# Four-batch attention with a routed feed-forward layer: VectorE's program nested in its branches, tile weights moved by transfers, name marks made on VectorE, expert work from step 53

## The chip, the cores and the metric

The kernel runs on one core of a Trainium2 chip. The metric is the device time of one execution in microseconds (us), smaller is better. The times shown are a median of three runs; one further execution was recorded by the hardware profiler, and every row below is from that one.

## The reference

Four sequences of 1024 tokens, 128 features each, go through a layer norm. The result is used twice, and both uses are added to the input.

```
xn  = layernorm(x)                                   # x is 4 x 1024 x 128
# attention, 16 heads of 8 features
Q, K = rope(xn @ W_q.T), rope(xn @ W_k.T);  V = xn @ W_v.T
attn = softmax(Q K^T / sqrt(8));            a = (attn V) @ W_o.T
# feed-forward: 8 experts, each token takes its 2 best
w, idx = top_k(xn @ Wg, 2);  w = softmax(w)
h_e   = relu((xhat * gamma_e + beta_e) @ W1_e + b1_e)     # 128 -> 512
out_e = h_e @ W2_e + b2_e + xn                            # 512 -> 128
y     = sum over the two experts of w * out_e
return x + a + y
```

## The kernel before, in words

The attention is a loop of 256 **steps**, counted by n: 4 batches of 64 steps, each batch 4 **quads** of 16 steps (a quad is four heads), each quad two halves of 8 steps (512 queries), and a step takes one block of 128 keys. In step n TensorE computes the scores of step n + 1 (line L631, into `sc`), then one piece of other work, called an **aside**, and then weighs the values with the exponentials of step n (L665, into `acc`). ScalarE does the two exponentials of each step (L879, into `ring`). At every step that 8 divides VectorE runs `tail`: it transposes `acc` (L1048) and so releases it; the weighing of that step waits for this. VectorE's own part of the asides, in the order of `aside(n)`, comes behind the tail. Each engine runs its program strictly in the order written, and all PSUM traffic of the asides goes through one bank, `aside_bank`, one piece at a time, by the counters `bank_full` and `bank_taken`.

Which aside stands at which step is a table of numbers. Up to step 26 the asides prepare the values and the routing. Then `mark` (VectorE, L1180 and L1182) makes one-hot matrices for the routing in 8 groups; GpSimd multiplies the narrow one by row and pair names (`named`, L456 and L458); `invert` on TensorE (L692) turns each group into part of a list, which VectorE adds up (`take_named`, L1190 and L1193); `tokens` (L1199 to L1212) makes from the list the numbers of the rows that each of the 71 tiles of 128 token slots gathers. From step `FFN_FROM` on two asides serve one tile: `layer_one` (TensorE L710, VectorE `relu` L1251) and `layer_two` (TensorE L699 for the next tile's transpose and L720, VectorE `rows_out` L1258 with `columns` L1245). They are spread evenly over the steps up to 236, apart from steps that other asides take. A tile's weights (1158 floats a partition: two matrices, biases, gamma and beta) are copied by VectorE from `w_all`, where all experts lie, into one of three buffers `w_tile` in the memory of `xn` (L1240; the expert's number is read into a register at L1237). GpSimd gathers the token rows (L483) and scatters the results (L493) by indirect transfers, and adds up and splits the rotated projections of the next batch (`split`, L466 to L472), which ScalarE squares for a bound (L885). SyncE loads the score operands of the next quad (`load_stack`, L310).

The bound decides, once for a batch, whether the slow path with row maxima is needed; with these inputs it never is. TensorE's program is nested: the fast path of all batches stands in a row, the slow paths behind it. VectorE's before has a test ahead of every quad, which jumps over `maxima` when the path is fast: 16 taken branches.

## Time and profile before

| | us |
|---|---|
| median of 3 runs | 644.51 (643.55 to 647.97) |
| the profiled execution, its own time | 650.07 |
| its span, first to last instruction | 648.2 |

The profiled execution is 5.56 us longer than the median. Sums are made against it, and then carried to the median.

### The profile page before, as it was taken

Reading aid. Unit: us, or ns where it says so; the run is one execution under the profiler, and the core shown is the slowest. Engines: PE = TensorE matmul, PEld = TensorE weight load, DVE = VectorE, ACT = ScalarE, POOL = GpSimd, SP = SyncE. Lnnn points to the kernel's source line nnn. Section 1 sums busy time; section 2 is a strip of 40 time slices with the busy share of each in tenths; the row PEclk is TensorE's granted clock in tenths of the full one; section 3 lists DMA queues with packets and bytes.
Section 4 is the critical chain, followed back from the end, with each engine's and each line's share of the span. In section 5 each row is a group of like instructions: output and inputs, shape, how many; then the busy total and the mean of one; then the engine's idle time right before and its main releaser. Section 6 shows DMA issues by size and latency. Waiting matters only on the chain.

```text
span 648.2 us, 12158 instructions
## 1 busy us (share of the span) xinstructions
PE 574.3 (89%) x4620; PEld 242.5 (37%) x4620; DVE 358.3 (55%) x1057; ACT 504.7 (78%) x552; POOL 277.5 (43%) x319
## 2 busy tenths in 40 slices
PE   8899865898999999899989999989998999989783
PEld 6233111234444444244434444434433544434111
DVE  4965879565554444667545444466654445334661
ACT  3799976777788888678857888777876888868991
POOL 4399547599643233456422323336632323311000
PEclk9999989889999999899979999999998999989996
DMA  6167310001101101000120100100022011110720
GB/s 233 34 184 210 98 34 1 4 22 54 55 22 45 34 25 50 18 17 26 50 54 18 51 29 25 50 17 22 22 58 51 21 54 26 35 37 10 295 84 18
DMA packets 25362, 35.48 MB, mean 55 GB/s; under 512 B 5440, under 2 KB 15728, under 8 KB 24784
## 3 DMA queue, kind: packets, MB, share of 16 engines
q1 hardware_dynamic: 19936, 23.70, 11.9%
q0 software_dynamic: 4544, 9.32, 5.3%
q10 hardware_dynamic: 816, 1.61, 0.7%
q8 instruction: 39, 0.64, 0.4%
q14 instruction: 27, 0.22, 0.1%
HBM read 17.36 MB, written 8.85 MB: 40 GB/s over the span
## 4 chain that ended last, share of the span: by engine, by line
PE 68%; DVE 15%; ACT 9%; issue 4%; DMA 2%; another core or an unknown queue 1%; ACTq 1%; POOL 0%; DVEq 0%
PE acc L665 27%; PE aside_bank L710 12%; PE aside_bank L720 10%; PE sc L631 10%; ACT ring L879 9%; PE aside_bank L699 3%; DVE work L1251 2%; DVE blocks L1048 2%; DVE xn L1240 2%; PE aside_bank L558 2%; PE aside_bank L729 2%; DMA sin<-rope_sin 1%; DVE rotated L1221 1%; PE aside_bank L542 1%; DVE turned L921 1%
## 5 line engine op out<-in xcount | busy, mean ns | idle before, releaser
L879 ACT ACTIVATE ring<-sc 128x1024 f32<-128x1024 f32 x512 | 490.6, 1039 | 112.8 <-PE sc L631 96.6
L665 PE MATMUL acc<-ring,v 128*9 128x512 f32 x2048 | 275.3, 608 | 51.3 <-DVE blocks L1048 33.1
L483 POOL DMA_INDIRECT work<-normed,token x71 | 71.9, 1013 | 230.5 <-DVE work L1245 224.9
L1251 DVE TENSOR_SCALAR work<-aside_bank,xn 128x128 f32<-128x128 f32 x284 | 80.0, 344 | 124.8 <-PE aside_bank L710 113.8
L631 PEld LDWEIGHTS sc<-qs,ks 32*128 32x128 f16 x1024 | 25.9, 91 | 230.9 <-ACT ring L879 180.7
L631 PE MATMUL sc<-qs,ks 32*128 32x512 f16 x1024 | 102.9, 390 | 4.0 <-ACT ring L879 2.0
L493 POOL DMA_INDIRECT token_out<-work,token x71 | 72.9, 1027 | 45.2 <-DVE work L1245 22.3
L710 PE MATMUL aside_bank<-work,xn 128*128 128x128 f32 x568 | 82.7, 289 | 2.0 <-DVE rotated L1221 2.0
L720 PE MATMUL aside_bank<-xn,work 128*128 128x128 f32 x568 | 77.4, 280 | 0.0
L710 PEld LDWEIGHTS aside_bank<-work,xn 128*128 128x128 f32 x568 | 69.4, 192 | 18.6 <-issue 18.6
L720 PEld LDWEIGHTS aside_bank<-xn,work 128*128 128x128 f32 x568 | 73.9, 202 | 0.3 <-DVE work L1251 0.3
L665 PEld LDWEIGHTS acc<-ring,v 128*9 128x9 f32 x2048 | 30.7, 88 | 102.8 <-DVE blocks L1048 31.7
L1240 DVE COPY xn<-w_all 128x1158 f32 x71 | 62.7, 883 | 0.3 <-issue 0.3
L1258 DVE TENSOR_TENSOR work<-aside_bank,xn 128x128 f32<-128x128 f32 x71 | 20.7, 291 | 70.8 <-PE aside_bank L720 70.8
L1048 DVE STREAM_TRANSPOSE blocks<-acc 128x512 f32<-128x512 f32 x32 | 22.8, 711 | 24.2 <-PE acc L665 22.8
L1245 DVE TENSOR_SCALAR work<-aside_bank,xn 128x128 f32<-128x128 f32 x71 | 28.5, 402 | 1.5 <-PE aside_bank L699 1.5
L699 PE MATMUL aside_bank<-const,work 128*128 128x128 f32 x71 | 22.2, 313 | 4.1 <-DMA work<-normed,token 2.1
L456 POOL TENSOR_SCALAR xn<-xn,const 128x568 bf16<-128x568 bf16 x8 | 15.6, 1955 | 23.7 <-DVE xn L1182 23.7
L921 DVE SCALAR_TENSOR_TENSOR turned<-aside_bank,gain,cos 128x512 f32<-128x512 f32 x13 | 9.7, 749 | 16.9 <-PE aside_bank L558 16.9
L451 POOL TENSOR_SCALAR xn<-xn,small 128x128 f32<-128x128 f32 x32 | 18.6, 605 | 0.1
L699 PEld LDWEIGHTS aside_bank<-const,work 128*128 128x128 f32 x71 | 10.0, 140 | 21.4 <-issue 12.0
L466 POOL TENSOR_TENSOR turned<-turned,rotated 128x512 f32<-128x512 f32 x12 | 15.9, 1326 | 0.2
(185 smaller groups left out, 369.0 us busy)
## 6 DMA issues: line engine op xcount, KB each, us to landing
w_all<-L_ffn_W SPq DMA_DIRECT2D x16, 256.0 KB, 4.8
qs<-hl SPq DMA_DIRECT2D x60, 64.0 KB
ks<-hl SPq DMA_DIRECT2D x60, 64.0 KB
x<-L_attn_x SPq DMA_DIRECT2D x4, 512.0 KB, 8.3
normed<-xn SPq DMA_DIRECT2D x4, 512.0 KB, 3.3
xn<-token_out SPq DMA_DIRECT2D x2, 1024.0 KB, 5.8
w_all<-token_out SPq DMA_DIRECT2D x2, 1024.0 KB, 10.9
out<-x SPq DMA_DIRECT2D x8, 256.0 KB, 2.2
```

Source lines behind the costliest of these rows:

```text
L483: pool.indirect_dma_start(out=xt[t % TILE_BUFFERS], out_offset=None, in_=xh_d[:, :], in_offset=bass.IndirectOffsetOnAxis(ap=token[:, 0, t: ...
L493: pool.indirect_dma_start(out=y_d[:, :], in_=ys[done % TILE_BUFFERS], in_offset=None, out_offset=bass.IndirectOffsetOnAxis(ap=token[:, 1, ...
L631: last = nc.tensor.matmul(dst, ks[r:r + 32, kb * P:(kb + 1) * P], qs[r:r + 32, at], start=True, stop=not slow)
L665: last = nc.tensor.matmul(acc[32 * j:32 * j + VW, :], v9[:, b, kb, 4 * g + j, :], ring[:, (2 * n + j // 2) % UNITS, j % 2, :], start=(kb = ...
L699: return nc.tensor.transpose(bank[0][:, D:D + P], xt[t % TILE_BUFFERS], ident)
L710: last = nc.tensor.matmul(bank[0][:, c * P:(c + 1) * P], w_tile[t % 3][:, c * P:(c + 1) * P], xsT[t % 2], start=True, stop=True)
L720: last = nc.tensor.matmul(bank[0][:, 0:D], hT[t % 2][:, c, :], w_tile[t % 3][:, W2_AT + c * D:W2_AT + (c + 1) * D], start=(c == 0), stop=( ...
L879: nc.scalar.activation(ring[:, (2 * n + u) % UNITS, :, :], sc[score_pair(2 * n + u)][:, :].rearrange("p (h c) -> p h c", h=2), ACT.Exp, sc ...
L1048: nc.vector.transpose(blocks[:, :, :].rearrange("p q r -> p (q r)"), acc[:, :]).then_inc(acc_out, 1)
L1240: nc.vector.tensor_copy(w_tile[t % 3], w_all[:, bass.ds(e, 1), :].rearrange("p o w -> p (o w)")).then_inc(w_ok, 1)
L1245: return nc.vector.tensor_scalar(xsT[t % 2], bank[0][:, D:D + P], w_tile[t % 3][:, GA_AT:GA_AT + 1], w_tile[t % 3][:, BE_AT:BE_AT + 1], AL ...
L1251: last = nc.vector.tensor_scalar(hT[t % 2][:, c, :], bank[0][:, c * P:(c + 1) * P], w_tile[t % 3][:, B1_AT + c:B1_AT + c + 1], 0.0, ALU.ad ...
```

## The change

Five things are changed together.

1. VectorE's program gets the nesting that TensorE's has: with the fast path, no branch is taken between the start and the end of the loop, and one far jump stands at its end. The flag of the next batch is read after step 62 of the batch, by TensorE too (it was 61).
2. VectorE's copies of the tile weights are gone. SyncE reads the expert's number and issues a transfer from `w_all` into `w_tile`: three at step 49 (steps are counted as above), then the one of tile t + 3 at the step of `layer_two(t)`.
3. GpSimd's `named` products are made by VectorE, behind each `mark`.
4. The table is new: experts from step 53 (48), `invert` at 34 to 49 (33 to 44), `tokens` at 49 (45), `gates` at 46 (26), and small moves of projections and bounds.
5. The same number of expert asides (142) goes into 184 steps in place of 189.

```diff
-ROUTE_AT, RANKS_AT, SLOTS_AT, GATES_AT = 21, 24, 24, 26
-INVERT_AT = {33 + (3 * g + 1) // 2: g for g in range(GROUPS)}
+ROUTE_AT, RANKS_AT, SLOTS_AT, GATES_AT = 21, 24, 24, 46
+INVERT_AT = {n: g for g, n in enumerate((34, 36, 39, 41, 43, 45, 47, 49))}
-TOKENS_AT = 45
-PLAIN_AT = {n: (1, r) for r, n in enumerate((37, 43, 46, 50))}
+TOKENS_AT = 49
+PLAIN_AT = {n: (1, r) for r, n in enumerate((38, 44, 48, 51))}
-BRANCH_AT = 61
+BRANCH_AT = 62
-FFN_FROM, FFN_TO = 48, 237
-NORM_AT = {PER_BATCH * b - 8: b for b in range(1, B)}
-FLAG_AT = {PER_BATCH * b - 6: b for b in range(1, B)}
+FFN_FROM, FFN_TO = 53, 237
+NORM_AT = {PER_BATCH * b - 6: b for b in range(1, B)}
+FLAG_AT = {PER_BATCH * b - 4: b for b in range(1, B)}
-SQUARE_AT.update({n: (1, r) for r, n in enumerate((50, 51, 53, 55))})
+SQUARE_AT.update({n: (1, r) for r, n in enumerate((50, 55, 56, 57))})
-WEIGHTS_AT = {n: t + 2 for n, t in FIRST.items() if t + 2 < SLOT_TILES}
+WEIGHTS_AT = {n: t + 3 for n, t in SECOND.items() if t + 3 < SLOT_TILES}
...
+            def weights(t):
+                e = sp.value_load(owner[0:1, t:t + 1], min_val=0, max_val=E - 1)
+                if t >= 3:
+                    sp.wait_ge(bank_taken[0], USE["two", t - 3])
+                sp.dma_start(w_tile[t % 3], w_all[:, bass.ds(e, 1), :].rearrange("p o w -> p (o w)")
+                             ).then_inc(w_in[t % 3], 16)
...
+                    if n == TOKENS_AT:
+                        sp.wait_ge(exp_in, 16 * 3 * E)
+                        sp.wait_ge(owner_ok, 1)
+                        sp.wait_ge(bank_taken[0], USE["invert", GROUPS - 1])
+                        for t in range(3):
+                            weights(t)
+                    if n in WEIGHTS_AT:
+                        weights(WEIGHTS_AT[n])
...
-            for g in range(GROUPS):
-                k, js = g % 2, slice(GROUP * g, GROUP * (g + 1))
-                pool.wait_ge(mark_ok, g + 1)
-                nc.gpsimd.tensor_scalar(named[k][:, :, 0, :], tile_mark[k], row_name, None, ALU.mult
-                                        ).then_inc(named_ok, 1)
-                nc.gpsimd.tensor_tensor(named[k][:, :, 1, :], tile_mark[k],
-                                        pick_name[:, js].unsqueeze(2).to_broadcast([P, GROUP, SLOT_TILES]), ALU.mult
-                                        ).then_inc(named_ok, 1)
...
-                pe.wait_ge(named_ok, 2 * (g + 1))
...
-                pe.wait_ge(w_ok, t + 1)
+                pe.wait_ge(w_in[t % 3], 16 * (t // 3 + 1))
...
+                link(nc.vector.tensor_tensor(tile_mark[k], iota_t[:, 0:SLOT_TILES].unsqueeze(1).to_broadcast(shape),
+                                             slot_hl[:, 0, js].unsqueeze(2).to_broadcast(shape), ALU.is_equal))
+                nc.vector.tensor_scalar(named[k][:, :, 0, :], tile_mark[k], row_name, None, ALU.mult)
+                nc.vector.tensor_tensor(named[k][:, :, 1, :], tile_mark[k],
+                                        pick_name[:, js].unsqueeze(2).to_broadcast(shape), ALU.mult
                                         ).then_inc(mark_ok, 1)
...
-            def weights(t):
-                e = v.value_load(owner[0:1, t:t + 1], min_val=0, max_val=E - 1)
-                if t >= 3:
-                    v.wait_ge(bank_taken[0], USE["two", t - 3])
-                nc.vector.tensor_copy(w_tile[t % 3], w_all[:, bass.ds(e, 1), :].rearrange("p o w -> p (o w)")
-                                      ).then_inc(w_ok, 1)
...
-            for b in range(B):
-                v.wait_ge(flag_ok, b + 1)
-                fast = v.value_load(flag[0:1, b:b + 1], min_val=0, max_val=1)
+            def attend(b, slow):
+                following = None
                 for n in body_steps(b):
-                    if (n + 1) % PER_QUAD == 0:
-                        with v.If(fast == 0):
-                            maxima((n + 1) // PER_QUAD)
+                    if slow and (n + 1) % PER_QUAD == 0:
+                        maxima((n + 1) // PER_QUAD)
                     if n >= 0:
                         aside(n)
+                    if not slow and n == PER_BATCH * b + BRANCH_AT and b + 1 < B:
+                        following = flag_of(b + 1)
+                return following
...
+            def batches(b, fast):
+                links = chain[0]
+                with v.If(fast == 1):
+                    following = attend(b, False)
+                    if b + 1 < B:
+                        batches(b + 1, following)
+                chain[0] = links
+                with v.Else():
+                    for later in range(b, B):
+                        attend(later, True)
```

Three places of the program, before and after. The first is VectorE behind the slots, where the first two groups are marked. `small` belongs to `gates`, `xn` holds the marks, `wide_q` to `mrow` are the slow path. Before:

```order
L1120 TENSOR_SCALAR small<-small 128x32
L1180 TENSOR_TENSOR xn<-const,slot_hl 128x1024
L1182 TENSOR_TENSOR xn<-const,slot_hl 128x568
L1180 TENSOR_TENSOR xn<-const,slot_hl 128x1024
L1182 TENSOR_TENSOR xn<-const,slot_hl 128x568
L1339 COMPARE_AND_BRANCH
L1029 TENSOR_SCALAR wide_q<-qs,missing 128x1024
L1030 CAST wide_k<-ks 128x1024
L1033 TENSOR_REDUCE mx<-sc 128x1 x32
L1036 TENSOR_SCALAR mrow<-sc 32x128
L1039 TENSOR_SCALAR mrow<-mrow 32x128
L1042 TENSOR_TENSOR mrow<-mrow 32x128
```

After:

```order
L1177 CAST slot_hl<-slot_i 128x128
L1188 TENSOR_TENSOR xn<-const,slot_hl 128x1024
L1190 TENSOR_TENSOR xn<-const,slot_hl 128x568
L1192 TENSOR_SCALAR xn<-xn,const 128x8x71
L1193 TENSOR_TENSOR xn<-xn,const 128x8x71
L1188 TENSOR_TENSOR xn<-const,slot_hl 128x1024
L1190 TENSOR_TENSOR xn<-const,slot_hl 128x568
L1192 TENSOR_SCALAR xn<-xn,const 128x8x71
L1193 TENSOR_TENSOR xn<-xn,const 128x8x71
L1055 STREAM_TRANSPOSE blocks<-acc 128x512
```

The seven `small` instructions of the gates have gone to step 46, two products stand behind each pair of marks, and the tail (the last row) follows without the slow path between.

The second is VectorE in an expert step ahead of a tail, at step 103 before (`work` is the relu's output, `owner` the expert's number):

```order
L1251 TENSOR_SCALAR work<-aside_bank,xn 128x128 x4
L1237 TENSOR_LOAD owner
L1237 ISA x2
L1240 ISA
L1240 COPY xn<-w_all 128x1158
L1048 STREAM_TRANSPOSE blocks<-acc 128x512
L1051 RECIPROCAL rec<-blocks 128x16
L1052 TENSOR_TENSOR att<-blocks,rec 128x16x8
```

After, at the same tail:

```order
L1255 TENSOR_SCALAR work<-aside_bank,xn 128x128 x4
L1262 TENSOR_TENSOR work<-aside_bank,xn 128x128
L1249 TENSOR_SCALAR work<-aside_bank,xn 128x128
L1055 STREAM_TRANSPOSE blocks<-acc 128x512
L1058 RECIPROCAL rec<-blocks 128x16
L1059 TENSOR_TENSOR att<-blocks,rec 128x16x8
```

The read of the owner and the copy are gone; here the second layer's two instructions stand ahead of the tail.

The third is SyncE after step 54 (`qs` and `ks` are the score operands of the next quad). Before, these transfers follow one another with only tests between:

```order
L310 DMA qs<-hl 32x1024 x4
L310 DMA ks<-hl 32x1024 x4
L365 TENSOR_LOAD flag
L365 ISA x2
L369 COMPARE_AND_BRANCH
```

After:

```order
L351 DMA xn<-w_all 128x1158
L311 DMA qs<-hl 32x1024 x4
L311 DMA ks<-hl 32x1024 x4
L348 TENSOR_LOAD owner
L348 ISA x2
L351 ISA
L351 DMA xn<-w_all 128x1158
```

The weights' transfers now stand in SyncE's program between the loads for the quads, in order with them.

## Rows read from the trace of the kernel before

**Rows 1.** Three stretches: start:end, length, busy us (x count) by engine, clock, DMA, GB/s.

```profile
0.00:143.60 143.60, 120.04 (x905) 44.62 (x906) 101.71 (x363) 109.34 (x136) 94.93 (x128) 0.96 0.31 92
143.60:599.00 455.40, 422.55 (x3472) 190.86 (x3476) 232.74 (x618) 360.31 (x378) 182.34 (x192) 0.98 0.13 35
599.00:648.20 49.20, 31.67 (x249) 7.05 (x248) 23.82 (x77) 35.04 (x38) 0.27 (x1) 0.88 0.34 131
```

**Rows 2.** Chain of waits in time order: start, length, what.

```profile
354.12 1.09 PE aside_bank L710 x8
359.04 1.09 PE aside_bank L710 x8
...
599.06 27.59 ACT ring L879 x30
```

**Rows 3.** Groups by line from 0 to 143.6 us: busy, mean ns, idle before.

```profile
L879 ACT ACTIVATE ring<-sc 128x1024 f32<-128x1024 f32 x106 | 100.5, 1050 | 19.1 <-PE sc L631 16.0 <-issue 2.7
...
L710 PE MATMUL aside_bank<-work,xn 128*128 128x128 f32 x16 | 2.9, 340 | 0.3 <-DVE rotated L1221 0.3
```

**Rows 4.** Who waited for whom from 143.6 to 599 us: total, times, longest.

```profile
PE acc L665 <- DVE blocks L1048: 24.3, 15, 2.8
```

**Rows 5.** VectorE's groups by shape, whole span.

```profile
L1240 DVE COPY xn<-w_all 128x1158 f32 x71 | 62.7, 883 | 0.3 <-issue 0.3
...
L1182 DVE TENSOR_TENSOR xn<-const,slot_hl 128x568 bf16<-128x568 f32 x8 | 8.7, 1093 | 0.0
```

**Rows 6.** Timeline of VectorE and TensorE around the first marks, 84 to 114 us.

```profile
84.54 0.17 DVE L1114 TENSOR_SCALAR small<-small 128x32 f32<-128x32 f32 x1
...
86.01 1.22 DVE L1180 TENSOR_TENSOR xn<-const,slot_hl 128x1024 bf16<-128x1024 f32 x1
87.15 0.74 DVE L1182 TENSOR_TENSOR xn<-const,slot_hl 128x568 bf16<-128x568 f32 x1
...
89.60 0.71 DVE L1048 STREAM_TRANSPOSE blocks<-acc 128x512 f32<-128x512 f32 x1
...
90.37 1.90 PE L665 MATMUL acc<-ring,v 128*9 128x512 f32 x8 [3.72 <-DVE blocks L1048]
...
113.12 1.30 PE L665 MATMUL acc<-ring,v 128*9 128x512 f32 x8 [3.93 <-DVE blocks L1048]
```

**Rows 7.** Timeline: TensorE's first expert tile waits for its gather.

```profile
130.41 0.30 PE L699 MATMUL aside_bank<-const,work 128*128 128x128 f32 x1 [2.09 <-DMA work<-normed,token]
```

**Rows 8.** Timeline: ScalarE's square of batch 1, last piece.

```profile
152.79 0.63 ACT L885 ACTIVATE xn<-turned 128x512 bf16<-128x512 f32 x1 [2.38 <-POOL turned L466]
```

**Rows 9.** Timeline: a weight copy ahead of a tail, and the weighing behind it.

```profile
268.06 1.90 DVE L1240 COPY xn<-w_all 128x1158 f32 x1
...
270.64 1.81 PE L665 MATMUL acc<-ring,v 128*9 128x512 f32 x8 [2.35 <-DVE blocks L1048]
```

**Rows 10.** Timeline at the start of batch 2, behind VectorE's branch.

```profile
327.69 1.16 PE L710 MATMUL aside_bank<-work,xn 128*128 128x128 f32 x8
...
330.45 1.13 DVE L1251 TENSOR_SCALAR work<-aside_bank,xn 128x128 f32<-128x128 f32 x4 [3.35 <-remote]
...
332.97 1.90 PE L665 MATMUL acc<-ring,v 128*9 128x512 f32 x8 [2.82 <-DVE blocks L1048]
```

**Rows 11.** Timeline at the start of batch 3, and at step 224.

```profile
492.24 1.54 PE L665 MATMUL acc<-ring,v 128*9 128x512 f32 x8 [2.00 <-DVE blocks L1048]
...
570.08 1.94 ACT L879 ACTIVATE ring<-sc 128x1024 f32<-128x1024 f32 x2 [2.45 <-remote]
```

**Rows 12.** TensorE's branches: ns min/median/max, first and last start.

```profile
L809 PEldq COMPARE_BRANCH  x5: 71/73/3279, 22.5 to 632.5; - x5
```

**Rows 13.** DMA issues: KB each, us from issue to landing.

```profile
xn<-token_out SPq DMA_DIRECT2D x2, 1024.0 KB, 5.8
...
ks<-hl ACTq DMA_DIRECT2D x2, 32.0 KB, 2.1
```

**Rows 14.** Timeline: VectorE near the end.

```profile
640.88 0.72 DVE L1048 STREAM_TRANSPOSE blocks<-acc 128x512 f32<-128x512 f32 x1 [10.99 <-PE acc L665]
```

More of the change, by code:

```diff
@@ L271, in build @@
         v_one, shift_zero, xh_out, ws_ok = (sem(n) for n in ("v_one", "shift_zero", "xh_out", "ws_ok"))
-        halves_ok, mark_ok, named_ok, token_ok = (sem(n) for n in ("halves_ok", "mark_ok", "named_ok", "token_ok"))
+        halves_ok, mark_ok, token_ok = (sem(n) for n in ("halves_ok", "mark_ok", "token_ok"))
         wqk_tr, wv_tr, wT_ok, wvg_ok, wo_sorted = (sem(n) for n in ("wqk_tr", "wv_tr", "wT_ok", "wvg_ok", "wo_sorted"))
@@ L284, in build @@
                                                                          "owner_ok"))
-        base_ok, w_ok, merged, out_ok = (sem(n) for n in ("base_ok", "w_ok", "merged", "out_ok"))
+        base_ok, merged, out_ok = (sem(n) for n in ("base_ok", "merged", "out_ok"))
+        w_in = [sem(f"w_in{k}") for k in range(3)]
         y_home = [sem(f"y_home{b}") for b in range(B)]
@@ L344, in _ @@
                 sp.dma_start(w_all[:, e, B2_AT:B2_AT + D], b2_d[e:e + 1, :].to_broadcast([P, D])).then_inc(exp_in, 16)
+            def weights(t):
[4 more added lines that the diff above has]
+                             ).then_inc(w_in[t % 3], 16)
             def load_outputs():
-                sp.wait_ge(w_ok, SLOT_TILES)
+                for k in range(3):
+                    sp.wait_ge(w_in[k], 16 * len(range(k, SLOT_TILES, 3)))
                 for k in range(TILE_BUFFERS):
@@ L1177, in mark @@
                     bank_is_full(0, "invert", g - 2)
+                    v.wait_ge(mark_ok, g - 1)
                 k, js = g % 2, slice(GROUP * g, GROUP * (g + 1))
@@ L1312, in aside @@
                 if n == FFN_FROM - 1:
-                    v.wait_ge(exp_in, 16 * 3 * E)
-                    v.wait_ge(owner_ok, 1)
-                    weights(0)
                     bank_is_full(0, "tile")
                     columns(0).then_inc(bank_taken[0], 1)
-                    weights(1)
                 if n in FIRST:
@@ L1322, in aside @@
                     rows_out(SECOND[n])
-                if n in WEIGHTS_AT:
-                    weights(WEIGHTS_AT[n])
                 if n in SINE_AT:
```

8 lines of the change are left out of this document (5 added, 3 removed).

## The prediction, made before the changed kernel ran

> **What bounds the kernel now.** I read the stretches first [rows 1]. From 143.6 to 599 us, the expert part, TensorE is busy 422.6 of 455.4 us (93%), VectorE only 232.7 and ScalarE 360.3: TensorE sets the pace. The chain of waits gives that pace: two steps of an expert tile take 359.04 - 354.12 = 4.92 us, 2.46 a step [rows 2]. Without expert work ScalarE sets it: 30 exponentials, 15 steps, in 27.59 us, 1.84 a step [rows 2]. So an expert aside costs 2.46 - 1.84 = 0.62 us wherever it stands, and 142 of them cost the same in 184 steps as in 189. VectorE's 62.7 us of weight copies [rows 5] therefore lie almost wholly beside TensorE's work, and most of what the change removes is worth nothing. What can be won is in places where TensorE stands still for VectorE: at the tails, 24.3 us in 15 waits in the expert part [rows 4], and more before it [rows 6].
>
> **Steps 32 to 52, where the table is new.** ScalarE has done 106 exponentials by 143.6 us, so step 53 begins there, and TensorE by then has begun two expert tiles (16 L710 records are two first layers) [rows 3]; by the table two second layers are behind it or running too. The weighing of step 32 waited 3.72 us for its tail, that of step 40 3.93 us, both times with VectorE deep in marks [rows 6]; the first tile waited 2.09 us for its gather [rows 7]. Now the same with the new order, with durations of rows:
> - A mark is 1.22 + 0.74 us when nothing disturbs it [rows 6], less some 0.1 of overlap. The two products are not on VectorE in this trace. The nearest row for the one of two tensors is L1182, same size, 0.74; for the one with a scalar between a third of that and 0.74, I take 0.4. With the wait between, a mark with names is 3.1 us (2.9 to 3.5). Before, beside GpSimd's products, L1182 took 1.09 in the mean against 0.74 [rows 5]; that disturbance goes, since GpSimd is then idle.
> - First tail: the gates, 84.54 to 86.01, move away (-1.5), two pairs of products come in (+2.5): the transpose starts near 90.7, not 89.60 [rows 6]. That is 1.1 us lost.
> - Later: mark plus `take_named` is 3.4 us, against two steps of 3.68. VectorE keeps up except where a projection with its sine (2.2 us) or a tail (1.3) falls between. I followed the three engines through steps 33 to 52 with these numbers. TensorE waits some 3 us at step 40 (as now), 1.3 near 46, 1.5 near 49, and a few tenths elsewhere. It no longer waits for GpSimd's chain of products. Step 53 begins near 138.5, 5.0 us earlier. Of this the four expert asides that had been done before and now are not, 4 x 0.62 = 2.5 us, must be given back later. Net -2.5.
> - Start of the expert part: tokens to first tile is now three steps, not two, so the 2.09 us wait [rows 7] would go (it is in the 5.0 above). But the gathers now meet three weight transfers of 593 KB. I charge +1.0 (0 to +4). Sum of this part: -1.5 us.
>
> **The square.** ScalarE stood 2.38 us for GpSimd's sum of the last projection of batch 1 [rows 8], since that split came two rounds of gathers and scatters late. The new table runs all three splits in round 3 and squares at step 57: -2.4.
>
> **Copies that collide ahead of a tail.** The copy at 268.06 took 1.90 us [rows 9], against a mean of 0.88 over all 71 [rows 5]; GpSimd's split ran at the same time, and I take the two to disturb each other; the tail stands behind it and TensorE 2.35 us behind that, then at a lower clock for a step (1.81 against 1.05 us) [rows 9]. The same happens once a batch later. Without the copy the transpose starts right behind the relu: -2.3 and -1.2, together -3.5.
>
> **VectorE's taken branches.** There are 16. At the start of batch 2 the relu starts at 330.45 where TensorE was through by 327.69 + 1.16 = 328.85: 1.6 us late, then a copy (0.76) and the tail; TensorE waits 2.82 and runs slow for one and a half steps [rows 10]. I put that at 3.8: the wait of 2.82, 0.85 on the first weighing (1.90 against 1.05), the rest on slow scores. Batch 3 has the same with a wait of 2.00 [rows 11]: 1.9. At the other 14 I find no late start of VectorE. So nesting pays at two of 16: -5.7 with the clock, of which the copies are a part. At its end the new program has one far jump. TensorE's took 3.28 us [rows 12]. VectorE has nothing to do for 10.99 us before its last transpose [rows 14], so I cost the jump at nothing; without that cover it would be +3.3.
>
> The Trainium skill ("Runtime: NRT & Kernel Launch", Instruction fetch mechanics) says that a taken branch stalls when its target is outside the two pages that are held. By that rule, the trace agrees: the far jump shows, most short ones don't. The rule speaks against the change, since 14 of the 16 branches that go were cheap and the one that comes is far; a sum that paid 1.6 us for each of 16 would give 22 us more than mine.
>
> **Copies ahead of other tails.** 24.3 us in 15 waits, less the 2.35, 2.82, 2.00 and their likes, leaves tails at which 0.76 of a copy was partly in the way: about -1.2. The step where both ScalarE and VectorE stood until 570 us, 2.45 us [rows 11], has no releaser that I can name. I leave it (0, range to -3).
>
> **The transfers.** 593 KB a tile. Bounds from rows: 32 KB landed in 2.1 us, 1024 KB in 5.8 [rows 13]; I take 4. A transfer goes out when `layer_two(t)` is taken and is asked for by `columns(t + 3)` two tiles later, 9.8 us. SyncE may be busy with eight loads of a quad in between, but these are there once in 16 steps. So it hides. The added traffic is 593 KB per about 5.1 us, 115 GB/s beside 35 [rows 1]. Gathers have three tiles in hand. I charge +1.0 for the whole (0 to +6).
>
> The Trainium skill ("DMA: Bandwidth & Descriptors", Issuing engines are not separate DMA queues) says that transfers of all issuing engines run on the same 16 DMA engines and interleave. By its fit (Anatomy of one DMA, 2.0 us plus bytes at 436 GB/s, for GpSimd's path) one of 593 KB is an estimated 3.4 us; the sum would be the same by it. No trace here has both streams together.
>
> **Sum.** -1.5 - 2.4 - 3.5 - 5.7 - 1.2 + 1.0 = -13.3 us. Against the profiled execution's own 650.07 that is 636.8. The median is 5.6 us shorter than that execution, so some of its stalls are probably not in every run; 644.51 - 13.3 = 631.2, and I give back a little: **632.0**. With the bounds: all of it, 570 us too and 2 us more from the table, 625; table nothing, branches half, transfers +6, about 642.
>
> **Rivals.**
> - *The weights come late.* Three buffers: a buffer is in use for one tile (4.92 us) and then waits for issue (0.6) and landing. A round of three tiles takes 14.76 us, so it decides from a landing of 9.2 us on. At 10.3 us every tile takes (10.3 + 0.6 + 4.92) / 3 = 5.27 us, 0.35 more; over 68 tiles 24 us, less the gain: 656. For: never has this core moved such a stream beside gathers and score loads. Against: 1024 KB landed in 5.8 [rows 13], and DMA load is 13% [rows 1]. Chance 0.07.
> - *VectorE becomes the bound in steps 32 to 52.* If the products take 1.09 each, as L1182 in the mean, every mark costs 0.8 to 1.0 more, eight marks 7 us, most of it seen. Together with a clock that drops after each stall: 639. Chance 0.12.
> - *The stalls are of the profiled execution.* If the two branch stalls and the clock dips are rare in plain runs, -5.7 falls to -1 and the collisions stay: 637 to 641. Chance 0.13.
> - *More than forecast:* the stall at 570 belonged to the branch or to a fetch of VectorE's, and the table gives its 5 us in full: 626. Chance 0.12.
> - *Every taken branch costs, hidden by other waits.* Were each of the other 14 worth the 1.6 us of batch 2 [rows 10], 22 us more would go: 610. The timeline, where 14 don't show, speaks against. Chance 0.02.
>
> **How the numbers follow.** The forecast (628 to 637) has 0.54. Range 624 to 643: it holds the forecast, the second, third and fourth rival, 0.91 by this list and less in truth, since the hand-followed part may be off by 3 us either way. 1% is about what a measurement of this kernel can tell from no change: below 638.1 is faster. Faster: 0.54 + 0.12 + 0.02 + half of the second and third (0.12) = 0.78. Within 1%: 0.14. Slower: the late weights, and something like a reaction of the clock, 0.08.
>
> **What would show each step.** Step 53's exponentials (the 107th) near 138 to 139 us; the tail of step 32 near 91; VectorE's products near 0.4 and 0.74 us and L1182's kin at 0.74 throughout; no wait of ScalarE for GpSimd's sum; relus of steps 127 and 191 within 0.1 us of TensorE's end; total wait of the weighing for tails in the expert part near 12 us instead of 24; weights landing in 3 to 6 us, no wait of TensorE or VectorE for them except at the first tile; the last transpose unmoved by VectorE's far jump. Wrong it would be if expert steps took more than 2.46 us all along, or if the first tile waited 5 us for gather or weights.

## The result, and the profile after

The changed kernel takes 619.88 us (618.98 to 620.08, 4 runs), against 644.70 (643.55 to 647.97, 4 runs) for the kernel before, run beside it: ratio 0.960, 95% interval 0.957 to 0.963. The gain is 24.8 us; the forecast was 12.5 and the range ended at 624. The profiled execution took 618.98, its span is 617.1.

The stretches of the kernel after, cut where [rows 1] are cut: at step 53's and step 237's first exponential. Columns: stretch, us, busy us of PE, PEld, DVE, ACT, POOL, clock, DMA share, GB/s.

```profile
0.00:139.10 139.10, 117.55 (x878) 41.08 (x878) 97.56 (x364) 108.29 (x135) 58.09 (x98) 0.95 0.33 101
139.10:571.50 432.40, 418.49 (x3498) 191.25 (x3502) 181.80 (x562) 358.89 (x379) 188.40 (x206) 1.00 0.37 132
571.50:617.10 45.60, 30.05 (x248) 6.92 (x248) 23.82 (x77) 35.05 (x38) 0.25 (x1) 0.91 0.36 142
```

Against [rows 1] the first stretch is 4.5 us shorter, the expert part 23.0 (455.4 to 432.4), and the end 3.6. TensorE does nearly the same work in the expert part (418.5 us busy, 422.6 before) and is now busy 97% of it. So the gain is idle time of TensorE. The wait of [rows 4] (24.3 us, 15 times) has almost gone; here are the three largest waits of TensorE in the expert part after (who waited for whom, total, times, longest). There is none for weights, only one for the first gather. The largest, for VectorE's relu, stands in the step behind a tail in four of its five places.

```profile
PE aside_bank L706 <- DVE work L1255: 3.7, 5, 1.5
PE acc L673 <- DVE blocks L1055: 2.6, 5, 0.5
PE aside_bank L706 <- DMA work<-normed,token: 1.6, 1, 1.6
```

The first marks, in the place of [rows 6], VectorE and TensorE:

```profile
84.75 1.23 DVE L1188 TENSOR_TENSOR xn<-const,slot_hl 128x1024 bf16<-128x1024 f32 x1
85.89 0.74 DVE L1190 TENSOR_TENSOR xn<-const,slot_hl 128x568 bf16<-128x568 f32 x1
86.67 0.37 DVE L1192 TENSOR_SCALAR xn<-xn,const 128x568 bf16<-128x568 bf16 x1
86.95 0.74 DVE L1193 TENSOR_TENSOR xn<-xn,const 128x568 bf16<-128x568 bf16 x1
...
90.47 0.71 DVE L1055 STREAM_TRANSPOSE blocks<-acc 128x512 f32<-128x512 f32 x1
...
91.23 1.90 PE L673 MATMUL acc<-ring,v 128*9 128x512 f32 x8 [4.46 <-DVE blocks L1055]
```

The reader sees the products at 0.37 and 0.74, and the transpose of step 32 at 90.47; the estimates were 0.4, 0.74 and 90.7.

### The profile page after: what moved, and what is told of

It reads as the page before. It is cut to its first block, busy times and chain, and to the rows that moved or that the text cites. A ratio compares the mean times of both kernels' runs of the same rounds, so it can differ in the third digit from the quotient of the medians.

```text
span 617.1 us, 12160 instructions
## 1 busy us (share of the span) xinstructions
PE 566.1 (92%) x4620; PEld 239.3 (39%) x4620; DVE 303.2 (49%) x1002; ACT 502.2 (81%) x552; POOL 246.7 (40%) x303
## 4 chain that ended last, share of the span: by engine, by line
PE 72%; ACT 13%; DVE 9%; issue 4%; DMA 1%; ACTq 0%; DVEq 0%
PE acc L673 28%; ACT ring L886 13%; PE aside_bank L717 12%; PE sc L639 10%; PE aside_bank L727 10%; PE aside_bank L706 3%; PE aside_bank L566 2%; PE aside_bank L736 2%; DVE work L1255 1%; DVE blocks L1055 1%; PE aside_bank L550 1%; DVE xn L1188 1%; DVE rotated L1232 1%; PE sc L566 1%; DMA wr<-L_attn_W_k 1%
## 5 line engine op out<-in xcount | busy, mean ns | idle before, releaser
L673 PE MATMUL acc<-ring,v 128*9 128x512 f32 x2048 | 271.4, 602 | 26.2 <-ACT ring L886 12.1
L501 POOL DMA_INDIRECT token_out<-work,token x71 | 71.1, 1001 | 42.4 <-DVE work L1249 19.4
L727 PE MATMUL aside_bank<-xn,work 128*128 128x128 f32 x568 | 75.1, 275 | 0.0
L727 PEld LDWEIGHTS aside_bank<-xn,work 128*128 128x128 f32 x568 | 71.4, 196 | 0.3 <-DVE work L1255 0.3
L673 PEld LDWEIGHTS acc<-ring,v 128*9 128x9 f32 x2048 | 30.5, 88 | 76.1 <-ACT ring L886 25.9
L566 PE MATMUL aside_bank<-xnT,wT 128*128 128x512 f32 x26 | 14.5, 641 | 1.4 <-DVE work L1204 0.8
L480 POOL TENSOR_TENSOR hl<-turned,hl 128x512 f16<-128x512 f32 x12 | 14.0, 1167 | 1.0
```

The lines of the kernel that those rows point to most:

```text
L501: pool.indirect_dma_start(out=y_d[:, :], in_=ys[done % TILE_BUFFERS], in_offset=None, out_offset=bass.IndirectOffsetOnAxis(ap=token[:, 1, ...
L566: return nc.tensor.matmul(dst, wT[:, k, :], xnT[:, b * S + c * CH:b * S + (c + 1) * CH], start=True, stop=True)
L673: last = nc.tensor.matmul(acc[32 * j:32 * j + VW, :], v9[:, b, kb, 4 * g + j, :], ring[:, (2 * n + j // 2) % UNITS, j % 2, :], start=(kb = ...
L727: last = nc.tensor.matmul(bank[0][:, 0:D], hT[t % 2][:, c, :], w_tile[t % 3][:, W2_AT + c * D:W2_AT + (c + 1) * D], start=(c == 0), stop=( ...
```

## The experiments

Fifteen kernels in four sets, each set with runs of the kernel before on its own chip. Medians of before were 646.97, 642.76, 642.22 and 642.04, so ratios carry across sets better than times. The changed kernel itself ran in none of the four sets: a difference from it in us, taken from two medians, can be off by some 3 us, and where the ratios give another number it stands beside. A single profile varies too. Its first exponential comes at 23.2 to 28.2 us in the 17 profiles, by nothing that was changed, and the expert part took 432.4, 432.1 and 429.4 us in three kernels with the same program there (after, branches_back, after_landing_142_on). One word on lines: where a kernel has more or fewer lines ahead of a place, the same instruction has another number (L665, L673 and L682 are the same weighing).

### One part undone

Each is the changed kernel with one part as it was.

**copies_back**

```diff
-                sp.dma_start(w_tile[t % 3], w_all[:, bass.ds(e, 1), :].rearrange("p o w -> p (o w)")
-                             ).then_inc(w_in[t % 3], 16)
...
+                nc.vector.tensor_copy(w_tile[t % 3], w_all[:, bass.ds(e, 1), :].rearrange("p o w -> p (o w)")
+                                      ).then_inc(w_ok, 1)
```

The waits for the weights and the steps at which they are asked for go back with it.

> The changed kernel with the weight copies back on VectorE; the table, the nesting and the names stay as changed. Theory A (free steps): the kernel gained mainly because the new table has 5 free steps at tails where the old had 15 and 3 more taken by other asides; a copy matters only at the few tails that it stands ahead of. Then this costs 4 to 8 us: 624 to 628. Theory B (copies): the copies ahead of the tails were the cost, whatever the table: 12 us or more back, 632 or above. Theory C (transfers dear): the 593 KB transfers cost something themselves, so this is no slower than 620.

Measured: 625.62 (623.89 to 627.84), ratio 0.968 (0.962 to 0.973).

**branches_back**

```diff
-            batches(0, flag_of(0))
...
+                    if (n + 1) % PER_QUAD == 0:
+                        with v.If(fast == 0):
+                            maxima((n + 1) // PER_QUAD)
```

> The changed kernel with VectorE's 16 tests and jumps back; all else as changed. Forecast's step: two late relus with what hangs on them, so 3 to 6 us slower, 623 to 626. Rival: the late relus need the copy behind them to be seen by TensorE, and without copies the branches cost under 1 us each: below 622. Rival: the nesting is the large part, 10 us or more: 630 or above.

Measured: 619.32 (617.42 to 620.94), ratio 0.959 (0.954 to 0.967). Sixteen tests and jumps on VectorE are worth nothing that shows, as the first rival said.

**names_back**

```diff
-                nc.vector.tensor_scalar(named[k][:, :, 0, :], tile_mark[k], row_name, None, ALU.mult)
+                nc.gpsimd.tensor_scalar(named[k][:, :, 0, :], tile_mark[k], row_name, None, ALU.mult
+                                        ).then_inc(named_ok, 1)
...
```

The second product goes back in the same way.

> The changed kernel with the names back on GpSimd, table as changed. VectorE's marks get 1.0 us shorter but disturbed by GpSimd again. Theory of the trace: the tail of step 32 comes 2.2 us earlier, but groups wait for GpSimd's 2.9 us chain; the new table leaves two steps (3.7 us) to each group, so it is about even: 618 to 622. Rival (the names' move was needed): marks of 2.6 to 3.1 us and TensorE waiting for names, 623 or above.

Measured: 615.48 (612.19 to 616.51), ratio 0.952 (0.945 to 0.958). The third part of the change costs 4.4 us by the medians (5.4 by the ratios), against an expectation of about even: step 53 begins at 134.7 in place of 139.1. By ScalarE's starts, steps 33 to 52 take 46.2 us here and 50.0 to 52.2 in the five kernels with the new table and the products on VectorE.

**after_free_at_tails**

```diff
+AT_TAILS = (64, 80, 88, 96, 104, 120, 128, 144, 152, 160, 168, 184, 192, 208, 216, 224, 232)
...
-    due = (n + 1 - FFN_FROM) * 2 * SLOT_TILES
+    due = (n + 1 - FFN_FROM) * 2 * SLOT_TILES + 5 * (FFN_TO - FFN_FROM)
-    if n not in TAKEN and used * (FFN_TO - FFN_FROM) < due:
+    if n not in TAKEN and n not in AT_TAILS and used * (FFN_TO - FFN_FROM) < due and used < 2 * SLOT_TILES:
```

> The changed kernel, but the free steps of the expert part lie at the same 17 tails as before (5 others at the end); the number of expert asides is the same. Theory A (a free step at a tail is partly lost, since TensorE has nothing to do while VectorE transposes): without copies each costs some 0.5 us, 12 more of them than in the changed kernel, so 6 us: 625 to 627; with copies it would be some 1.0 each. Theory B (copies alone): no change, 619 to 621.

Measured: 621.22 (619.53 to 621.80), ratio 0.961 (0.955 to 0.967): 1.3 us by the medians, 0.5 by the ratios, which is no difference that can be told, and not the 5 or more of theory A. The expert part of its profile is 434.8 us, 2.4 to 5.4 more than in the three profiles named above.

What follows: no part undone gives back more than 6 us, though 24.8 were won. Either the parts stand in for one another, or the gain is in the table.

### One part alone

Each is the kernel before with one part changed.

**table_alone**: the numbers of the new table, nothing else. 

> The kernel before with the new table of steps alone: copies on VectorE, names on GpSimd, tests ahead of quads, all as before. From the first four runs: the changed kernel 619.9, copies back +5.7, names back -4.4, branches back -0.6; if the parts add, this is 620.6. Theory A (the table is the large part): 618 to 625, some 22 us below the kernel before. Theory B (parts stand in for each other, each hides the tail's wait): 630 to 636.

Measured: 618.50 (615.81 to 618.91), ratio 0.960 (0.957 to 0.963). The table alone gives the whole gain.

**before_tails_filled**: one line of the code that makes the table; a step that 8 divides always gets an expert aside, and others are left free in its place.

```diff
-    if n not in TAKEN and used * (FFN_TO - FFN_FROM) < due:
+    if n not in TAKEN and (used * (FFN_TO - FFN_FROM) < due or n % KB == 0 and used < 2 * SLOT_TILES):
```

> The kernel before with one line changed: a step that 8 divides always gets an expert asides, and the free step comes right behind it. No other change. Theory A (a free step at a tail is lost with the copy in the way): 15 free steps at some 0.8 us, 10 to 14 us faster: 631 to 635. Rival (the tail costs the same with or without an aside beside it, since VectorE's relu then stands behind the tail): no change, 643 to 646.

Measured: 623.74 (623.11 to 626.82), ratio 0.971 (0.968 to 0.974): 19 us by one line, where 10 to 14 were expected. It also moved the place at which TensorE's far jump lands, which is worth 3 of them (see "Behind the last loop step").

**transfers_alone**: the edit of copies_back the other way round. 

> The kernel before with the weights moved by SyncE's transfers alone; old table, names on GpSimd, tests as before. Three transfers at step 45 and the first tile at step 47, so the first weights may be waited for some 3 us. If the copies' cost lies in tails as the trace of before had it (24.3 us in 15 waits, less those that stay), 12 to 16 us faster: 629 to 633. If it is only what undoing it in the changed kernel cost, 5.7 less those 3: 640 to 643.

Measured: 628.21 (626.98 to 629.49), ratio 0.976 (0.974 to 0.979): 14.5 us, within the 12 to 16 of the first reading.

**nested_alone**: the edit of branches_back the other way round. 

> The kernel before with VectorE's program nested, nothing else. The forecast said 5.7 us for the two late relus with what follows. Theory A (they need a copy ahead of the tail to be seen, and here it is there): 3 to 6 us faster, 639 to 642. Rival (worth nothing here too, as in the changed kernel, and the late relus have another cause): 643 to 646.

Measured: 641.90 (640.12 to 642.51, 10 runs), ratio 0.997 (0.995 to 1.000): about 1 us, not 3 to 6.

**transfers_tails_filled**: both of the two large ones. 

> The fourth corner of a square: the kernel before with the weights by transfers (alone 628.2) and with its tails filled (alone 623.7). Theory A (both take away the same wait, of a weighing for a tail that stands behind a copy): without copies the filled tails bring 0 to 1.5 us in the expert part, which takes 428 to 430 us, and what else the fill brings is the place of TensorE's landing, 2.5 to 3.5 us: 623.5 to 626. Theory B (the two are independent terms of -14.5 and -19): 609 to 611.

Measured: 619.10 (617.17 to 620.21), ratio 0.964 (0.961 to 0.967). As independent terms the two would give 609; they share some 10 us. But theory A gave 623.5 to 626, so the filling still brings more with transfers (9 us, of which 3 are at the end, see below) than theory A allows.

The expert part of four of them, by stretches: nested_alone, before_tails_filled, transfers_alone, transfers_tails_filled.

```profile
144.86:589.53 444.67, 416.53 (x3472) 188.15 (x3476) 232.03 (x618) 360.34 (x378) 182.77 (x192) 1.00 0.13 36
```

```profile
144.90:576.00 431.10, 416.05 (x3472) 188.07 (x3476) 229.63 (x618) 358.55 (x379) 181.73 (x192) 1.00 0.13 37
```

```profile
147.40:577.20 429.80, 415.03 (x3472) 188.22 (x3476) 177.97 (x550) 359.75 (x379) 174.08 (x188) 1.00 0.36 129
```

```profile
147.50:571.60 424.10, 415.11 (x3472) 188.18 (x3476) 177.73 (x550) 358.45 (x378) 174.02 (x188) 1.00 0.37 131
```

The same TensorE work (415 to 416.5 us) in 444.7, 431.1, 429.8 and 424.1 us. Filling takes 13.6 off with copies and 5.7 with transfers; transfers take 14.9 off alone and 7.0 when the tails are filled. (The first of the four is nested_alone and not before, whose profiled execution had stalls of its own; the nesting is worth some 1 us.)

### Where the filled tail pays: step 80

The three steps 80 to 82 hold the same work everywhere: a tail, the second layer of tile 12, the first of tile 13, and one free step. The kernel before, with step 80 free:

```profile
209.93 1.13 DVE L1251 TENSOR_SCALAR work<-aside_bank,xn 128x128 f32<-128x128 f32 x4 [1.87 <-PE aside_bank L710]
...
210.97 0.75 DVE L1240 COPY xn<-w_all 128x1158 f32 x1
211.64 0.71 DVE L1048 STREAM_TRANSPOSE blocks<-acc 128x512 f32<-128x512 f32 x1
...
212.41 1.04 PE L665 MATMUL acc<-ring,v 128*9 128x512 f32 x8 [1.30 <-DVE blocks L1048]
```

TensorE has only scores to do between two weighings, and VectorE does relu, copy and transpose in a row. The wait is 1.30. The same with transfers:

```profile
212.14 1.13 DVE L1261 TENSOR_SCALAR work<-aside_bank,xn 128x128 f32<-128x128 f32 x4 [1.78 <-PE aside_bank L727]
...
213.18 0.70 DVE L1065 STREAM_TRANSPOSE blocks<-acc 128x512 f32<-128x512 f32 x1
...
213.94 1.05 PE L682 MATMUL acc<-ring,v 128*9 128x512 f32 x8 [0.54 <-DVE blocks L1065]
```

And with the copy where it was but the second layer moved onto the tail (before_tails_filled):

```profile
211.09 0.75 DVE L1240 COPY xn<-w_all 128x1158 f32 x1
...
211.41 1.06 PE L720 MATMUL aside_bank<-xn,work 128*128 128x128 f32 x8
211.76 0.71 DVE L1048 STREAM_TRANSPOSE blocks<-acc 128x512 f32<-128x512 f32 x1
...
212.52 1.05 PE L665 MATMUL acc<-ring,v 128*9 128x512 f32 x8
```

The second layer runs while VectorE copies and transposes, and TensorE's wait is gone. From ScalarE's starts, steps 80 to 82 take 7.52 us before (208.75 to 216.27), 6.75 with transfers (211.05 to 217.80) and 6.80 filled (208.96 to 215.76). In these three steps the size is that of the copy, by either way.

Over all places a second loss shows. ScalarE runs one step ahead, so what a free step n brings shows in the starts up to step n + 3. From n to n + 3 three expert steps take 7.3 us. With the free step n away from a tail they take 6.36, in nested_alone and in transfers_alone alike (10 places each). With the free step at a tail they take 6.76 in the mean with transfers (15 places), and with the copy 7.43 at the usual place, 7.65 in the mean, where the collisions of steps 105 and 169 are in it. So a free step brings 0.9 us elsewhere, 0.5 at a tail, and nothing at a tail behind a copy. The copy costs 0.67 there (0.73 in the mean of the first two steps, 11 us in 15), and the tail itself 0.40. The second is what filling still brings with transfers: 0.39 to 0.41 us in most of the stretches of eight steps whose tail was free (steps 80 to 87: 17.97 and 17.57), and 15 x 0.40 = 6.0 for the 5.7 measured.

### The table again, both ways

**table_alone_free_at_tails**: the edit of after_free_at_tails on table_alone. 

> The kernel before with the new table, but with the expert work's free steps held at the 17 tails at which an earlier table has no expert aside; copies on VectorE, names on GpSimd, tests ahead of the quads. With the new table as it stands this program took 618.5. Theory A (a free step is worth 1 us anywhere but at a tail that stands behind a copy, and 17 such tails lose it): the one line that filled the tails of the kernel before was worth 19 us, so taking them away again gives 634 to 638, with waits of the weighing for VectorE's blocks in the expert part of 15 us or more, and step 53 within 0.5 us of 134.6. Theory B (the gain of the table comes from the steps below 53, from the later gates, list and projections): 618 to 622, waits under 9 us.

Measured: 624.09 (622.15 to 626.38), ratio 0.970 (0.967 to 0.973): 5.6 us lost and not 15, step 53 at 135.2, the weighings' waits for VectorE's blocks up to 15.8 us in 19. Neither theory's number. ScalarE's starts say why: of the 17 free steps at tails only 6 now stand behind a first layer, whose relu the copy follows; from n to n + 3 they take 7.47 us in the mean. Ten stand behind a second layer, which has no copy, and take 6.73. (The last, 232, has another free step ahead.) In the kernel before all 15 stand behind a first layer. Against 6.36 elsewhere that is 6 x 1.11 and 10 x 0.37, 10.4 us, less 2.6 by the same count for the five free tails of table_alone: 7.8, where the expert parts of the two profiles differ by 7.2 (442.6 and 435.4). So a free tail costs 0.4, and behind a copy 1.1. I had counted tails and not what stands ahead of them.

**old_table**: the changed kernel with the numbers of before. 

> The changed kernel with the table of before: nesting, weights by transfers, names on VectorE, experts from step 48, 142 asides in 189 steps. Theory A (transfers already free most tails, the table does the rest): the transfers alone gave 628.2; names on VectorE add 3 to 5 us, since they lengthen the time to the first tail and stand ahead of the list; nesting takes 1: 629 to 634. Theory B (parts add up as separate terms, the table worth 24 us): 619.9 + 24 = 644.

Measured: 632.37 (630.39 to 633.26), ratio 0.984 (0.982 to 0.987), as theory A said. The table is worth 12.5 us in the changed kernel by the medians (some 16 by the ratios) and 24 in the kernel before. By stretches the two compare so: to step 53 148.6 and 139.1, expert part 430.1 and 432.4, behind it 49.9 and 45.6. With transfers, then, the table wins before step 53 and at the end, and in between nothing that is clear of what single profiles differ by: it has four more asides to do there, and ten fewer free steps at tails.

### The order of the marks

**names_back_mark_later** is names_back with one number more:

```diff
-MARK_AT = {27: 0, 28: 1}
+MARK_AT = {27: 0, 32: 1}
```

> The changed kernel with the name products back on GpSimd and the second mark moved from step 28 to step 32, where VectorE runs it behind the tail. With the products back alone it took 615.5. Theory A (the tail of step 32 stands behind two marks, TensorE waits 3 us or more for it, and ScalarE sets the pace below step 53, so that this wait shows in full): the weighing of step 32 no longer waits, step 53 begins 1.5 to 3 us earlier than 134.65, and the time is 612.5 to 614. Theory B (VectorE is short of time up to step 50 whatever the order, the second mark only comes late and the list with it): 615 to 617, with the wait moved to steps 36 to 41.

Measured: 608.63 (607.59 to 610.10, 5 runs), ratio 0.948 (0.945 to 0.950). Theory A's direction, and more than it said: 6.9 us below names_back by the medians, though 2.6 by the ratios. It is 11 us faster than the changed kernel by the medians, 8 by the ratios. The marks:

```profile
86.76 0.71 DVE L1065 STREAM_TRANSPOSE blocks<-acc 128x512 f32<-128x512 f32 x1
...
87.53 1.04 PE L682 MATMUL acc<-ring,v 128*9 128x512 f32 x8 [0.64 <-DVE blocks L1065]
...
89.26 1.68 DVE L1199 TENSOR_TENSOR xn<-const,slot_hl 128x568 bf16<-128x568 f32 x1
```

The weighing of step 32 waits 0.64 us, against 4.46 in the kernel after. L1199, the second operation of a mark, takes 1.68 with GpSimd beside it and not 0.74, yet that costs less than the two products did on VectorE. By ScalarE's starts, steps 33 to 52 take 41.9 us; in the kernel after 52.2, in names_back 46.2. In the next run, whose program is the same up to step 53, they take 43.3, so 3 to 4 us are the mark's.

**names_back_later_filled**: that with the tails filled too. 

> The same, and the expert asides never leave a tail free (the five tails 88, 96, 144, 184 and 232 are filled, and other steps are freed in their place). Theory A (a free step at a tail is lost only where the tail is late, and with transfers it hardly is): the five are worth 0 to 1.5 us, so 611.5 to 614. Theory B (a free step at a tail is worth nothing in any case): 5 us, so 608 to 610.

Measured: 608.50 (605.68 to 608.88, 6 runs), ratio 0.946 (0.943 to 0.948): no difference that can be told in the medians. In the profiles the expert part is 2.0 us shorter (430.3 and 428.3), five tails at 0.4, which is just above theory A's 0 to 1.5; steps 33 to 52 are 1.4 longer, where nothing was changed. The absolute times of both theories were built on too late a start. These two beat both kernels.

### Behind the last loop step

The end of the chain of waits in the kernel before, from the last exponential (columns: start, us, what):

```profile
634.28 1.56 issue
635.84 0.89 PE acc L665
636.73 2.19 issue
638.93 1.93 PE acc L665 x7
```

And after:

```profile
606.76 1.63 issue
608.39 1.22 PE acc L673 x8
```

TensorE has just come through its far jump [rows 12]. Before, it then does one of the last eight weighings and pauses 2.19 us; after, it doesn't pause. The four programs that have before's table and nothing moved on TensorE (before, nested_alone, transfers_alone, old_table) all show one and seven, with pauses of 2.19 to 2.43 us; no other program does.

**before_landing_12_on** and **after_landing_142_on** move only the place where the jump lands, by waits that are never run (24 here, by my count 12 instructions; 284 in the other, 142 instructions):

```diff
                 with pe.Else():
                     for later in range(b, B):
                         attend(later, True)
+                    for _ in range(24 if b == 0 else 0):
+                        pe.wait_ge(flag_ok, 1)
```

> The kernel before, with 24 waits more (12 instructions) at the end of TensorE's slow path, which is never run: they only move the place at which TensorE's far jump lands 12 instructions on, to where it stood in the kernel before with its tails filled. Theory A (behind its far jump TensorE fetches instructions once more, and whether it has to depends on the place of landing): in all four programs of before's table and length the first of the last eight weighings runs alone, and the other seven follow after an issue pause of 2.2 us; with 12 instructions more the eight run together. So the pause is gone, the span behind step 255 is 12.0 to 13.3 us and not 15.9, and the time is 2 to 3.5 us less, ratio 0.995 to 0.997. Theory B (the pause comes from the state of the memory or the clock at the end of these programs): nothing changes, ratio 1.00. The Trainium skill (Runtime: NRT & Kernel Launch, Instruction fetch mechanics) says that instructions are fetched in blocks of 256; A would agree with it.

Measured: 638.92 (636.89 to 641.06, 12 runs), ratio 0.995 (0.993 to 0.997): 3 us, and the pause is gone.

```profile
625.85 2.06 issue
627.91 1.94 PE acc L665 x8
```

> The changed kernel, with 284 waits more (142 instructions) at the end of TensorE's slow path, never run. It has 31429 TensorE instructions ahead of the place of landing, the kernel before 31315; with 142 more it is 31571, which is 256 more than before's place. Theory A: the pause of 2.2 us behind the first of the last eight weighings appears, the chain shows them as one and seven, and the time is 2 to 3.5 us more than the changed kernel's 619.9: 622 to 623.5. Theory B: 619 to 620.5. That 256 instructions are one block of fetching is what the Trainium skill says (Runtime: NRT & Kernel Launch, Instruction fetch mechanics).

Measured: 616.93 (616.63 to 619.17, 5 runs), ratio 0.963 (0.960 to 0.966), the eight in one piece. So where the jump lands does matter, but the pause doesn't come back 256 instructions on, and here theory A was wrong.

What the pause is made of, the DMA packets of the traces show. The profile counts them by queue; this is before's row for the instructions (kind: packets, MB, share).

```profile
q8 instruction: 39, 0.64, 0.4%
```

All 39 are of 16,384 bytes, and two stand behind the far jump: in before from 633.38 to 634.26 us and from 636.49 to 637.64, in before_landing_12_on from 625.46 to 626.34 and from 628.51 to 629.68. The second comes 3.1 us behind the first in both. In before TensorE stands from 636.73 to 638.93, until 1.3 us after that packet has ended (1.3 to 1.4 in the other three programs with the pause). In the other it weighs from 627.91 to 629.85, while the packet is still under way. That fits a TensorE that runs out of fetched instructions in the one program and not in the other, which is theory A. The Trainium skill (Runtime: NRT & Kernel Launch, Instruction fetch mechanics) has blocks of 16 KiB, 256 instructions. The size of the packets agrees. That the pause should come back one block on isn't borne out by after_landing_142_on, or my count of 31315 and 31429 isn't the chip's; that stays open.

## Why the prediction was wrong

**What held.** The time forecast for the first exponential of step 53 was 138.5; it came at 139.13, though by two errors that nearly cancel (see below). The square (-2.4): steps 54 to 56, by ScalarE's starts, went from 9.05 to 6.52 us. The copies that collide with GpSimd's split (-3.5): steps 105 and 106 went from 7.68 to 4.27 with transfers alone, 169 and 170 from 6.09 to 4.27, together -5.2; that they were the copies' was right and the term 1.7 too small. No wait for weights, at a DMA share of 0.37: the first rival fell. (When each landed, the trace doesn't record. The added stream was 97 GB/s and not 115: a tile took 6.1 us of the expert part and not 5.1.) The last transpose stayed behind TensorE, not behind VectorE's far jump.

**The step that failed** is the term for the copies ahead of other tails ("leaves tails at which 0.76 of a copy was partly in the way: about -1.2"), and the sentence it rests on, "an expert aside costs 2.46 - 1.84 = 0.62 us wherever it stands, and 142 of them cost the same in 184 steps as in 189". The 24.3 us in 15 waits of [rows 4] had been read rightly and then priced wrongly. I looked at the few waits that were long and took the rest for what a tail costs anyway. All 15 waits stand at the 15 free steps at tails, each but the last (step 232, 0.54 us) behind a copy. Five of them the prediction had taken up elsewhere (2.35 and 2.36 with the collisions, 2.82 and 2.00 with the branches, 2.76 at 570 us); the other ten are 12.0 us, priced at 1.2. Its own sign was "near 12 us instead of 24" of such waiting, and 2.6 were left. An aside's price of 0.62 was too low as well, and not the same wherever it stands: leaving it out brings 0.9 us away from tails, 0.5 at a tail, nothing at a tail behind a copy. The copy cost 0.73 x 15 = 11 us, the collisions' share at two tails included, and the free tails themselves 0.40 x 15 = 6. Both ways out are in the change. Transfers shorten the wait. The new table makes it rare: 189 steps for 142 asides leave a free step every fourth step, in step with the tails at every eighth, and 15 of 26 free steps fell on tails; 184 steps leave 5 of 22 there, and of these 3 behind a second layer. In before_tails_filled, which alters nothing in the expert part but that, 13.6 us went there (against nested_alone). The four asides given back were to cost 2.5 us, and old_table and the kernel after do differ by 2.3 in the expert part; but that difference holds the ten free tails fewer too, so the match is luck.

**A term that wasn't there:** the end, 0 in the sum, -3.1 in before_landing_12_on. The pause stands in the trace of before, but with no releaser, and I had read on from [rows 12] to [rows 14] without it.

**A term that was too large:** -5.7 for VectorE's branches. nested_alone gives -0.9. The two stalls of [rows 10] and [rows 11] aren't the branches'. Two things speak for that. In the profile of before itself each of the 16 took 56 to 67 ns, where TensorE's far jump took 3279 in the same kind of row [rows 12]:

```profile
L1339 DVEq COMPARE_BRANCH  x16: 56/56/67, 29.3 to 597.8; - x16
```

And before_landing_12_on has all its branches, and its relu at the same place starts with the idle time of any other:

```profile
329.21 1.13 DVE L1253 TENSOR_SCALAR work<-aside_bank,xn 128x128 f32<-128x128 f32 x4 [1.78 <-PE aside_bank L710]
...
331.73 1.05 PE L665 MATMUL acc<-ring,v 128*9 128x512 f32 x8 [1.25 <-DVE blocks L1050]
```

1.78 us behind TensorE's first layer and not 3.35; the 1.25 that is left is the copy's wait at a free tail. Steps 127 to 130 take 9.93 us there and in nested_alone, and 14.20 in the profiled execution of before; steps 191 to 194 9.93 and 12.21; steps 224 to 226, with the stall until 570 us, 7.43 and 10.54. So 9.7 us of that execution were stalls of its own. The third rival had this right, but its time of 637 to 641 left the rest of the sum as it was. By the Trainium skill (Runtime: NRT & Kernel Launch, Instruction fetch mechanics) a taken branch stalls when its target is outside the two pages that are held; 16 that are worth 1 us together show no such stall. Why the profiled execution stalled isn't known.

**A cost that was booked as a gain:** the products on VectorE. I took away GpSimd's chain and its disturbance of L1182 and found step 53 earlier. It was, but by the table: steps 33 to 52 take 56.9 us before, 47.2 in table_alone and 52.2 in the kernel after. So the table won 9 to 10 us there, of which the four asides moved out are 3.6 at 0.9 each, and the products took some 5 back (4 to 6 by the profiles of names_back's paragraph); the hand-followed net of 5.0 hid both. Against TensorE's wait for GpSimd stands the time at which the tails of steps 32 and 40 come: 4.46 us of waiting in the kernel after, 2.44 in names_back, at the first of them.

**The sum once more,** by the profiles of nested_alone (span 638.9) and the kernel after (617.1): steps 33 to 52 -4.0, the expert part -12.3, from step 237 on -3.8, of which 2.3 are the pause. That is -20.1, and the nesting itself some -0.9, against 22 measured from an undisturbed before (642 in three of the four sets). Of the 12.3, how much is the square's 2.5 and how much the copies', the tails' and the four asides' isn't added up term by term: the three profiles of one program differ by 3 us there. One sum of the prediction is also off in itself: its chances for "faster" add up to 0.80, not 0.78.

## What to carry to other kernels

A free slot is worth most where no other engine is late: put work of the engine that sets the pace on the steps where it would wait, and leave free those where it wouldn't. When two periodic patterns meet (free steps every fourth, tails every eighth), work out their phase from the table, and what stands ahead of each, before pricing either. Price a free slot over as many steps as its effect lasts: over two steps the tail's own 0.4 us didn't show. Sum up a wait that comes 15 times at 1 us before turning to one that comes twice at 2.8, and look whether a stall comes again in a second profile before giving it a cause.

## What the runs showed of the hardware

- Behind a far jump of TensorE (3.28 to 3.77 us in these traces) a second pause of 2.2 to 2.4 us can follow one group of matmuls later. It depends on the place of landing: 12 instructions more in a path that is never run took it away, 3.1 us in 642. In the trace a packet of 16,384 bytes on an instruction queue starts 3.1 us behind the jump's own, and the pause ends 1.3 to 1.4 us after it. A change of table can take such a pause away by accident, and here did.
- In the expert part transfers of 579 KB a tile (the 593 of the prediction, in units of 1024 bytes), 132 GB/s in all with the gathers, scatters and score loads, cost TensorE no wait that the trace shows.
- VectorE's product of two bf16 operands (128x568) took 745 ns in the mean and the comparison of the same size on f32 745 ns too; with a scalar the product took 374. With GpSimd's products beside it the comparison took 1093 in the mean in the kernel before [rows 5].
